# Moving the values matmuls forward in TensorE's written order of a step

## What is computed

```python
x = x + tanh(g_xattn[0]) * xattn(layernorm(x), ctx, ctx)
x = x + tanh(g_ffn[0]) * ffn(layernorm(x), wg, W, b)

def xattn(q, k, v):          # q, k, v: (16, 128, 512)
    qh = q.reshape(b * h, 16, 512); kh, vh alike
    qk = einsum('bdm,bdn->bmn', qh, kh) / sqrt(16)
    return einsum('bmn,bcn->bcm', softmax(qk, axis=-1), vh)

def ffn(x, wg, W, b):        # one expert of 8 for each of 2048 tokens
    probs = softmax(x @ wg); idx = argmax(probs)
    return probs[idx] * (x @ W[idx].T + b[idx])
```

## Time and profile before

| what | value |
|---|---|
| median of three executions | 651.05 us |
| the profiled execution | 653.81 us |
| its span, first to last instruction | 652.2 us |
| mean granted TensorE clock | 0.962 |
| TensorE matmuls busy | 542.4 us (83%) |
| VectorE busy | 448.6 us (69%) |
| ScalarE busy | 350.3 us (54%) |
| POOL busy | 370.7 us (57%) |
| maximum pass, maxima on VectorE (L801) | 512 of 681 ns |
| exps on ScalarE (L726) | 256 of 1023 ns |
| prologue, up to the first scores | 57 us |
| the 16 batches | 57 to 527 us |
| expert stage | 527 to 652 us |

### The profile page before, as it was taken

The page is one execution under the profiler, slowest core; times in us unless marked ns, Lnnn a source line. Parts: engine busy times, 40 slices in busy tenths (PEclk is TensorE's granted clock), DMA queues, the critical chain, the costliest instruction groups (busy, mean ns, idle before and its releaser), DMA issues. The chain is left out here.

```text
span 652.2 us, 9589 instructions
## 1 busy us (share of the span) xinstructions
PE 542.4 (83%) x2603; PEld 183.4 (28%) x2603; DVE 448.6 (69%) x883; ACT 350.3 (54%) x429; POOL 370.7 (57%) x631
## 2 busy tenths in 40 slices
PE   0177989898999989899998989897869699389993
PEld 0011222232323223232322323232212155145551
DVE  5486788888888888888997878888956634101110
ACT  2112777677777767877776676865537621011110
POOL 5442648858585765858577575864542634424441
PEclk9999999999999999999999989999979879879997
DMA  4754375666667567664465665373410235233310
GB/s 144 178 156 147 76 179 152 176 169 177 186 160 215 152 179 171 167 190 109 141 165 105 164 115 167 75 143 78 95 53 2 87 124 163 73 116 114 118 65 0
DMA packets 35045, 85.52 MB, mean 131 GB/s; under 512 B 10232, under 2 KB 10364, under 8 KB 34976
## 3 DMA queue, kind: packets, MB, share of 16 engines
q1 hardware_dynamic: 22848, 59.46, 37.0%
q0 software_dynamic: 12160, 25.62, 12.1%
HBM read 62.56 MB, written 27.15 MB: 138 GB/s over the span
## 5 line engine op out<-in xcount | busy, mean ns | idle before, releaser
L801 DVE TENSOR_REDUCE neg_max<-ps_ring 128x1 f32<-128x512 f32 x512 | 332.0, 681 | 67.3 <-PE ps_ring L1129 62.9
L726 ACT ACTIVATE probs<-ps_scores 128x1024 f32<-128x1024 f32 x256 | 251.5, 1023 | 103.0 <-PE ps_scores L1147 98.4
L1129 PE MATMUL ps_ring<-stacks 96*128 96x512 bf16 x512 | 200.9, 406 | 58.8 <-DMA stacks<-parts_dram 30.0
L1147 PE MATMUL ps_scores<-stacks 128*128 128x512 bf16 x512 | 156.7, 389 | 19.5 <-DMA stacks<-shift_parts 11.1
L1166 PE MATMUL ps_pv<-probs,v_ones 128*32 128x512 f32 x1024 | 141.1, 624 | 0.0
L1129 PEld LDWEIGHTS ps_ring<-stacks 96*128 96x128 bf16 x512 | 49.5, 97 | 256.2 <-DVE neg_max L801 206.3
L1223 PE MATMUL ps_scores<-w_sb,f_xt 128*128 x184 | 85.2, 607 | 0.0
L1147 PEld LDWEIGHTS ps_scores<-stacks 128*128 128x128 bf16 x512 | 47.9, 102 | 64.9 <-ACT probs L726 17.8
L519 POOL DMA_DIRECT2D stacks<-shift_parts x96 | 50.0, 523 | 20.3 <-POOL shift_parts L512 18.0
L719 ACT COPY f_xt<-ps_scores 128x512 f32<-128x512 f32 x23 | 13.4, 586 | 86.4 <-PE ps_scores L1206 86.4
L444 POOL TENSOR_SCALAR rs<-mv 128x1 f32<-128x1 f32 x32 | 6.0, 187 | 90.6 <-DVE mv L817 45.3
(11 more groups left out here) (139 smaller groups left out, 479.1 us busy)
## 6 DMA issues: line engine op xcount, KB each, us to landing
parts_dram<-prep POOLq DMA_DIRECT2D x16, 768.0 KB
stacks<-parts_dram SPq DMA_DIRECT2D x64, 192.0 KB
stacks<-parts_dram SPq DMA_DIRECT2D x64, 128.0 KB
w_sb<-w_t SPq DMA_DIRECT2D x16, 512.0 KB, 8.6
recs_dram<-rec SPq DMA_DIRECT2D x16, 512.0 KB, 11.8
prep<-x_perm SPq DMA_DIRECT2D x16, 256.0 KB, 5.0
prep<-k_perm SPq DMA_DIRECT2D x16, 256.0 KB, 8.8
v_in<-v_t SPq DMA_DIRECT2D x16, 256.0 KB
```

The lines of the kernel that those rows point to most:

```text
L726: nc.scalar.activation(probs[:, k % 2, 2 * jp:2 * jp + 2], ps_scores[:, jp], ACT.Exp).then_inc(exp_done, 1)
L801: nc.vector.tensor_reduce(neg_max[:, g, j, c:c + 1], ps_ring[:, u.slot(n)], AX.X, ALU.max, negate=True).then_inc(ring_free, 1)
L1129: nc.tensor.matmul(ps_ring[:, u.slot(n + c)], q_stack[0:KS, B.p, g, j, c * 128:(c + 1) * 128], k_stack[0:KS, B.p, g, j], start=True, stop= ...
L1147: last = nc.tensor.matmul(ps_scores[:, jp, j % 2], k_stack[0:KA, B.p, g, j, c * 128:(c + 1) * 128], q_stack[0:KA, B.p, g, j], start=True, ...
```

## The change

V moves from behind S1, R1 and R2 to the place behind R0 (and behind M, where there is one), and R1 moves ahead of S1. Before, a step was S0 R0 [M] S1 R1 R2 V [rank, turn_rows] R3 [route]. Now it is S0 R0 [M] V R1 S1 R2 [rank, turn_rows] R3 [route]. The numbers of the ring's turns stay as they were.

```diff
--- before.py
+++ after.py
@@ -1251,14 +1251,17 @@
                     if k == NC and nxt:
                         turn_maxima(B.plus(1), u, n, 0)
                         n += 1
-                    scores(B, k, 1)
-                    if nxt:
-                        scores_for_max(B.plus(1), u, n - 1, k, (1, 2))
-                        n += 2
                     if k > 0:
                         values(B, k - 1)
                     elif prev:
                         values(B.plus(-1), STEPS - 1)
+                    if nxt:
+                        scores_for_max(B.plus(1), u, n - 1, k, (1,))
+                        n += 1
+                    scores(B, k, 1)
+                    if nxt:
+                        scores_for_max(B.plus(1), u, n - 2, k, (2,))
+                        n += 1
                     for group in range(2):
                         if k == 3 and B.known(ROUTED[group]):
                             pe.wait_ge(high_read, B.b)
```

## The result

| | before | after |
|---|---|---|
| median of 4 executions | 651.47 us | 684.69 us |
| lowest and highest | 650.95, 657.06 | 681.45, 687.40 |
| the profiled execution, and its span | 653.81, 652.2 us | 681.45, 679.8 us |
| mean granted TensorE clock | 0.962 | 0.954 |

The ratio is 1.0499, interval [1.0458, 1.0541]: slower by 33.2 us, where the forecast was 16.2. The sign and the place of the new wait are as forecast; the size is twice it.

A forecast was written before the change was run, and what follows sets the result against it. It took a dependence loop between TensorE and VectorE (3.15 us a step) as the bound. Batches 2 to 9 12.8, 10 to 12 1.8, 13 and 15 1.6 made 16.2 on 653.8: 670.0 (667.3 against the median); range 657 to 685 us.

The forecast's parts named there:

- An ordinary step at nothing: Ordinary steps: the loop holds the same members, so the step stays at 3.15 us; cost 0, bounds 0 to 0.6 a batch.
- ScalarE's slack: Ordinary step: V now waits for later exps; slack was over a step and is now 0.15 us.
- V(0)'s wait: Batch start: V of step 0 waits for VectorE's logits copy, holding what stands behind it; loss 1.6 us a batch.
- the rest of the batch: After the batch start: shorter and longer stretches come to 0; the period of 28.23 us becomes 29.8.
- the clock: TensorE behind the new 1.4 us pause: no fall, cost 0; upper bound some 1.5 us a batch.
- Rival A: Clock falls at the new pause in most of 11 full-wait batches: 11 x 1.5 more, 684 us; chance 0.14.
- 206 us of such short waits: TensorE in the trace so far: these waits left ordinary steps at full clock, speaking against clock swings.
- Batches 10 to 12 and 13: Shift rows' DMA sets the step-4 scores in 10 to 12: 0.6 late each; batch 13's waits hide it: 0.3.
- Batch 15: Last batch: V stands between an exp and S1, delaying the gates' exp; at most 1.7 us, taken as 1.3.
- C: Rival, faster: V fills TensorE while VectorE catches up and R3 no longer waits; 649 down to 628 us; chance 0.08.
- D: Rival, no change: V of step 0 would have to find the logits copied; chance 0.04 with the like.
- B: Rival, most loss absorbed: POOL's chain sets step 4's S0 in batches 2 to 9 too; 659 us; chance 0.16.

The follow-up runs named there:

- the gates later: Kernel after with VectorE's gate arithmetic of the first routed group moved from step 5 to step 6, in batch 9 alone: 672.74 us, ratio 1.0442.
- steps 0 and 1 alone: Kernel before with the new order in steps 0 and 1 alone: 667.40 us, ratio 1.0362.
- the filled pause: Kernel after with six matmuls, their output overwritten, put ahead of V of step 0: 669.89 us, ratio 1.0341.
- the half filling: Kernel after with three overwritten matmuls in place of six ahead of V of step 0: 670.28 us, ratio 1.0357.
- step 1 alone new: Kernel before with the new order in step 1 of every batch alone: 652.99 us, ratio 1.0087.
- step 1 alone old: Kernel after with the old order in step 1 of every batch alone: 659.49 us, ratio 1.0197.

## Why the prediction was half right

- **An ordinary step at nothing: right.** 3.15 measured, by its timeline. ScalarE's slack, put at 0.15, sufficed.
- **V(0)'s wait: right.** Pause 1.33 to 1.42 (said 1.4), V(0) at M +5.56 to 5.65 (5.59), aggregate at M +4.09 (4.07), the transpose's wait for POOL gone, M to M 29.53 undisturbed (29.8). The experiments divide this loss further: 0.8 goes when the logits come early, 0.5 with the order of steps 0 and 4. It is 1.3 a batch and not 1.6: M of step 0 to M of step 4 grew by 1.58 (14.87 to 16.45), as said, but the rest of the batch came out 0.24 shorter (13.36 to 13.12), where I had its parts cancel. Over 8 batches that is 2.4 too much.
- **The step that failed** is the clock: "*after 1.43 us V took its full-speed 1.07 in batch 13. The new pause, 1.4, is nearest to the second, so I take 0.*" The price on the edge of my range, 1.5 a fall, was right (1.45), and the number of falls, taken as none, was wrong: 5 of 11 in the profiled execution, 7, 6 and 3 of 11 in the other three with the same pause (the kernel after again, the gates later, steps 0 and 1 alone), 21 of 44 in all. One row at 1.43 was one case where both outcomes occur, and I read it as the far side of a limit. By the filled pause the falls cost 1.6%, some 10 of the 17 us that the sum lacked. Rival A had the mechanism and, at 684, the time; but it reached the 684 by falls in every batch, which did not happen. That it met the 684.69 is luck: about half of its falls came, and batches 9, 13 and 14 made up for the rest. The trace's "206 us of such short waits" spoke of pauses of some 0.5 us, and these do leave the clock alone, by the half filling as well.
- The Trainium skill (TensorE: Matmul & The Clock Gate, "A second HAM failure mode: psum-queue depth-cycling") has short idle times between groups of matmuls tip the clock. The runs bear it out at 1.33 to 1.42, in half of the cases; at 0.5 to 0.6 they don't.
- **A term that was missing** is batch 9. I said that nothing but waits moves, and priced no operation by where it now falls against POOL. The cast went from 0.17 to 2.73: 2.6 us in one place, gone when the gates' chain was moved. It isn't the new V(0)'s doing: nine traces have the long cast (2.73 to 2.87), among them those with step 1 alone new and with step 1 alone old, and their batch 9 takes 33.4 to 35.6, where the kernel before has 28.26. TensorE idles 2.7 to 2.9 behind it.
- The Trainium skill (SBUF — State Buffer, "Who interferes with whom") describes the ports that VectorE shares with GpSimd as an exclusive lock, held for a whole instruction. The cast agrees with it in so far as it ends within 0.04 of POOL's second subtraction in all nine traces. It also began 0.42 before the first of them, while POOL was still issuing DMAs, and was held over both, which a lock for one instruction does not account for. That it is the port, and not another resource of the two engines, was not isolated.
- **Batches 10 to 12 and 13**: said +0.6 each and +0.3, measured +1.13, -1.26, +1.03 and +2.08. The shift rows' release moved by more than the aggregate, and in batch 13 V(0) has a fall behind a pause of 0.95 for which the sum has nothing. Batch 14, said 0, was +2.34, with a fall at the same place. **Batch 15**: the gates' exp stands at M +8.77 (534.06) against +7.38, +1.39 where I said 1.3; but from M to the end of the span it is only 0.5 longer (154.0 to 154.5), so most of it was absorbed by the expert stage or lies within how much this stretch varies (151.2 to 154.6 in all the traces).
- **The rivals**: C is out (no step under 3.14), D is out, and B too: POOL's chain sets nothing in batches 2 to 9, since the wait at the transpose is gone.

With the falls at one half, 11 x 0.5 x 1.5 = 8 us, and the cast, 2.6, the sum of 16.2 would have been 27: near the 27.6 of the profiled execution, and 6 under the medians' 33.2. That is nearer than the parts were: 2.4 too much in batches 2 to 9 stands against 4.1 too little in batches 13 and 14.

## What to carry to other kernels

In an in-order queue the instruction that may wait must stand where its input is ready with some tenths to spare; price what stands behind it, and try moving the producer (here one copy on VectorE) before the consumer. A pause of a microsecond or more on TensorE has two prices, its length and a chance of a slow clock behind it: count both, take the chance from several rows and not from the nearest one, and test it by filling the pause with idle matmuls. After a change of timing look also for small VectorE operations that now fall on a POOL operation, and look in every variant: the same cast was long in nine of the fourteen traces here, and it is easily booked to whatever the variant was made to test.

## What the runs showed of the hardware that was not expected

- The granted clock is no function of the pause before it alone. Behind V(0)'s pause it fell after 1.33 to 1.42 us in 21 of 44 cases, after 0.92 to 1.01 in 8 of 21 (3 of 13 with step 1 alone new; 5 of 8 in batches 13 and 14 of the four kernels with the long pause), after 0.51 to 0.61 in 0 of 11. Behind the 2.7 to 2.9 us for the long cast it fell in 6 of 9. A fall costs 1.0 to 1.6 us of a batch.
- A cast of 8 columns took 2.73 to 2.87 us in place of 0.17 in nine traces, and ended within 0.04 of POOL's second subtraction in each.
- Matmuls whose result is thrown away made a kernel 1.6% faster (1.034 against 1.050), three of them as well as six (1.036).
- A wait of 1.0 us per batch cost 0.0 to 0.1 us in one order of the steps, and an order with one of 1.4 cost 1.3, of which 0.8 went with the wait: what the steps behind a stall let VectorE catch up counts as much as the stall.
- V in halves of its columns takes 0.58 us each, where the whole takes 1.00.
